# Last graphs of a graph network: biases carried as a matrix row, first product by groups ahead of the last gates, another order of the final operations

## The reference, cut to what matters

```python
A = (adj != 0)
h = x
for l in range(5):                      # block one: message passing and a GRU
    m = h @ weight[l]
    agg = einsum('bij,bid->bjd', A, m)
    h = gru_cell(agg, h, w_ih, w_hh, b_ih, b_hh)   # h' = (1-z)*n + z*h
x = layernorm(x + h * mask)

fused = 0                               # block two: only nodes 0..24 of a graph
for g, idx in enumerate(GROUPS):        # five groups of node numbers below 25
    adj_g = adj[:, idx][:, :, idx]      # normalised by degrees in graph_conv
    h1  = relu(norm_adj @ (x[:, idx] @ W1[g]) + b1[g])
    out = relu(norm_adj @ (h1 @ W2[g]) + b2[g])
    fused[:, idx] += softmax(fusion_w)[g] * out
out = layernorm(x + fused)
```

## Time and profile before

| quantity | value |
|---|---|
| median of 3 runs | 494.8 us (494.42 to 495.2) |
| the profiled execution's own time | 494.57 us |
| its span, first to last instruction | 492.8 us |
| mean granted PE clock | 0.997 |
| PE busy | 482.4 us (98%) |
| DVE, ACT, POOL busy | 352.5, 303.3, 334.8 us |

### The profile page before, as it was taken

The page is one execution under the profiler, slowest core; times in us unless marked ns, Lnnn a source line. Parts: engine busy times, 40 slices in busy tenths (PEclk is TensorE's granted clock), DMA queues, the critical chain, the costliest instruction groups (busy, mean ns, idle before and its releaser), DMA issues.

```text
span 492.8 us, 7184 instructions
## 1 busy us (share of the span) xinstructions
PE 482.4 (98%) x2305; PEld 230.2 (47%) x2305; DVE 352.5 (72%) x663; ACT 303.3 (62%) x536; POOL 334.8 (68%) x378
## 2 busy tenths in 40 slices
PE   7999999999999999999999999999999999999995
PEld 5344444444444444444444444444444444564564
DVE  3777867696866687778687768868668675445796
ACT  4556655655655566777667776576755767645555
POOL 3654774748775598997689658659996766234466
PEclk9999999999999999999999999999999999999998
DMA  8878252665535447264955486223443233322313
GB/s 269 257 172 159 45 150 55 175 160 129 119 68 156 108 95 185 51 140 105 184 112 154 113 196 179 66 51 82 97 100 75 48 65 67 65 38 44 80 45 86
DMA packets 133732, 55.97 MB, mean 114 GB/s; under 512 B 97257, under 2 KB 125374, under 8 KB 133694
## 3 DMA queue, kind: packets, MB, share of 16 engines
q1 hardware_dynamic: 108316, 32.39, 32.3%
q10 hardware_dynamic: 25378, 23.12, 15.3%
HBM read 27.70 MB, written 4.19 MB: 65 GB/s over the span
## 4 chain that ended last, share of the span: by engine, by line
PE 82%; POOL 6%; DMA 4%; DVE 3%; issue 2%; ACT 2%; SPq 0%; POOLq 0%; DVEq 0%; ACTq 0%
PE pA L779 24%; PE pR L784 6%; PE pR L786 6%; PE pR L785 6%; PE pZ L786 6%; PE pZ L785 6%; PE pZ L784 6%; PE pIN L784 3%; PE pHN L784 3%; PE pIN L786 3%; PE pHN L785 3%; PE pIN L785 3%; PE pHN L786 3%; POOL ZH L515 2%; DMA HT<-NAT 1%
## 5 line engine op out<-in xcount | busy, mean ns | idle before, releaser
L526 POOL TENSOR_TENSOR HT<-H,HT 128x512 f16<-128x512 f32 x76 | 91.8, 1208 | 91.4 <-ACT HT L1149 91.4
L779 PE MATMUL pA<-A,NAT 128*128 128x512 fp8e4 x640 | 151.0, 379 | 0.0
L515 POOL TENSOR_TENSOR ZH<-Z,H 128x512 f32<-128x512 f32 (+1 forms) x80 | 102.6, 1282 | 28.7 <-ACT Z L1164 27.4
L1389 DVE SCALAR_TENSOR_TENSOR T<-pHN,BHN,R 128x512 f32<-128x512 f32 (+1 forms) x80 | 59.9, 748 | 78.5 <-ACT R L1156 78.1
L1169 ACT ACTIVATE pIN<-T,COLS 128x512 f32<-128x512 f32 (+1 forms) x80 | 55.3, 691 | 71.7 <-DVE T L1393 71.6
L779 PEld LDWEIGHTS pA<-A,NAT 128*128 128x128 f16 x640 | 62.3, 98 | 75.3 <-issue 1.5
L1149 ACT ACTIVATE HT<-H 128x512 f16<-128x512 f32 x76 | 47.8, 629 | 64.6 <-DVE H L1403 64.4
L1399 DVE SCALAR_TENSOR_TENSOR pIN<-Z,pIN 128x512 f32<-128x512 f32 (+1 forms) x80 | 55.1, 688 | 24.5 <-ACT pIN L1169 24.3
L1156 ACT ACTIVATE R<-pR,BRZ 128x512 f32<-128x512 f32 (+1 forms) x80 | 54.3, 679 | 22.4 <-PE pR L786 21.5
L1403 DVE TENSOR_TENSOR H<-ZH,pIN 128x512 f32<-128x512 f32 (+1 forms) x80 | 54.8, 685 | 10.0 <-POOL ZH L515 7.6
L1383 DVE TENSOR_TENSOR AG<-pA,AG 128x512 f16<-128x512 f32 x80 | 54.7, 684 | 8.1 <-ACT AG L1145 8.1
(11 more groups left out here) (288 smaller groups left out, 813.9 us busy)
## 6 DMA issues: line engine op xcount, KB each, us to landing
AS<-in_adj_dram ACTq DMA_DIRECT2D x13, 1024.0 KB, 5.9
XR<-in_x_dram ACTq DMA_DIRECT2D x16, 256.0 KB, 2.9
XS<-in_x_dram ACTq DMA_DIRECT2D x13, 256.0 KB, 3.6
out_dram<-Y SPq DMA_DIRECT2D x16, 192.0 KB, 2.3
AS<-in_adj_dram SPq DMA_DIRECT2D x2, 1024.0 KB, 8.8
AS<-in_adj_dram SPq DMA_DIRECT2D x4, 256.0 KB, 5.5
NAT<-HT SPq DMA_TRANSPOSE x64, 3.1
XS<-in_x_dram SPq DMA_DIRECT2D x3, 256.0 KB, 7.8
```

What stands on the lines that cost most here:

```text
L515: g_.tensor_tensor(ZH[:, cs], Z[:, cs], H[:, b, cs], ALU.mult).then_inc(zh_p, 1)
L526: g_.tensor_tensor(HT[:, b, 1, :], H[:, b, :], HT[:, b, 0, :], ALU.subtract).then_inc(h_lo, 1)
L779: last = mm(pA2[:, k % 2, :], NAT[:, k % 2, h, i, :], A8[:, b, i, :], start=(h == 0 and i == 0), stop=(h == 1 and i == NI - 1))
L1389: v.scalar_tensor_tensor(out=T[:, cs], in0=pHN[:, cs], scalar=BHN[:, 0:1], in1=R[:, cs], op0=ALU.add, op1=ALU.mult).then_inc(t_v, 1)
```

## The change

- **Biases.** `B2S` and `biases` go. The unused partition rows 96 to 127 of `S2` get the biases of `W2`'s layer in step 13; row 121 (`LAST_BIAS_ROW`) alone is kept, scaled with the fusion weight. `read_s` writes rows 0 to 120 only. A new matrix `BDT` is the adjacency plus, in row 121, the group's membership; it is made on DVE in step 40 by five operations. `conv_d` uses it.
- **Second stage by groups.** `conv_b(0)` does groups 0 to 2 for both hidden halves (6 matmuls for 5) and stands in PE's step 79 right behind the pHN product, ahead of the state's pR and pZ products. `conv_b(1)` does groups 3 and 4 (4 for 5). ACT's `read_b(0)` moves ahead of the reset gate of step 79.
- **Order of the end.** On PE, back(14) stands behind all the gates of step 79, and back(15) behind the whole first `conv_s`. On ACT, two blocks of graph 12 are normalised between the update gate and the tanh of step 79; graph 13's two between the two `read_s`. On DVE, scales(12) goes to step 79 and scales(13) ahead of new_state(79); scales(14) ahead of variances(15); `stats_z` behind scales(15) and normalise(15). `variances` has one operation less (L1471) and the POOL roots 4 elements for 5. On POOL, graph 13's blocks 0 and 1 are normalised instead of 2 and 3. The first store of graph 15 no longer waits for ACT.

```diff
@@ SP, store_y
-                sp.wait_ge(f_on, b + 1)
...
-                sp.dma_start(out[b, S:P, :], Y[S:P, b % 4, 0, :]).then_inc(st_y[b % 4], 16)
+                if b == B - 1:
+
+                    sp.dma_start(out[b, S:P, :], Y[S:P, b % 4, 0, :]).then_inc(st_y[b % 4], 16)
+                sp.wait_ge(f_on, b + 1)
+                if b < B - 1:
+                    sp.dma_start(out[b, S:P, :], Y[S:P, b % 4, 0, :]).then_inc(st_y[b % 4], 16)
@@ POOL
-                g_.tensor_tensor(RS[:, w, :], VE[:, w, :], NHALF[:, 0:NI + 1], ALU.pow).then_inc(f_rs, 1)
+                g_.tensor_tensor(RS[:, w, 0:NI], VE[:, w, 0:NI], NHALF[:, 0:NI], ALU.pow).then_inc(f_rs, 1)
...
             residual(B - 2)
+            pool.wait_ge(f_nb, E0 + 2)
             normalise(E0, range(2))
             inverse_root(B - 2)
-            normalise(E0 + 1, range(2, NI))
+            normalise(E0 + 1, range(2))
             inverse_root(B - 1)
@@ PE, gates_of_state
                 split_product(pHN[:, cs], WH[:, 0, 2, :], WH[:, 1, 2, :], ht[0], ht[1], True, True)
+                if k == K - 1:
+
+                    conv_b(0, LAST_BANKS[1])
                 if k > 0:
                     pe.wait_ge(sig_r, k)
                 split_product(pR[:, cs], WH[:, 0, 0, :], WH[:, 1, 0, :], ht[0], ht[1], True, False)
@@ PE
+            def conv_b(part, bank):
+                groups = LAST_PARTS[part]
+                n = COL[groups.stop] - COL[groups.start]
+                if part == 0:
+                    pe.wait_ge(c_ea, 1)
+                for g in range(groups.start, groups.stop):
+                    for h in range(NH):
+                        at = h * n + COL[g] - COL[groups.start]
+                        last = mm(bank[:, at:at + COL[g + 1] - COL[g]], W1S[:, g, h * P:(h + 1) * P],
+                                  YT[:, COL[g]:COL[g + 1]], start=True, stop=True)
                 last.then_inc(c_mm, 1)
@@ PE, the end
+            back(B - 2)
             conv_b(1, LAST_BANKS[2])
-            pe.wait_ge(sig_r, K)
-            biases(LAST_PARTS[0], LAST_BANKS[5][:, 0:3 * D])
-            pe.wait_ge(sig_z, K)
-            biases(LAST_PARTS[1], LAST_BANKS[6][:, 0:2 * D])
             pe.wait_ge(f_ym, B - 1)
             mm(FUT, IDF[:, :], X1[:, TAIL, :], start=True, stop=False)
+            pe.wait_ge(c_ea, 2)
+            conv_s(range(0, 3), LAST_BANKS[3])
+            back(B - 1)
             pe.wait_ge(c_ea, 3)
-            conv_s(range(0, 3), LAST_BANKS[3], lambda: back(B - 1))
             conv_s(range(3, G), LAST_BANKS[4])
+            pe.wait_ge(b2_v, 2)
+            pe.wait_ge(sig_r, K)
             pe.wait_ge(c_ea, 4)
-            conv_d(TAIL, range(0, 3), LAST_BANKS[5], True)
+            conv_d(range(0, 3), LAST_BANKS[5])
@@ ACT, step 79 and the end
                     read_a(TAIL, LAST_BANKS[0])
+                    read_b(0, LAST_BANKS[1])
                 reset_gate(k)
                 update_gate(k)
...
-                    read_b(TAIL, 0, LAST_BANKS[1])
+                    normalise(E0, range(2, NI))
                 new_gate(k)
...
+            act.wait_ge(b2_v, 1)
+            read_s(0)
+            normalise(E0 + 1, range(2, NI))
+            read_s(1)
+            read_d(0)
+            read_d(1)
             normalise(B - 2, range(2))
             normalise(B - 1, range(2, NI))
@@ DVE
+            def last_matrices():
+                dve.wait_ge(bd_p, BD_STEPS - 1)
+                for g in range(G):
+                    last = v.scalar_tensor_tensor(out=BDT[:, g, :, :], in0=CM[:, g:g + 1, :].to_broadcast([P, Q, S]),
+                                                  scalar=IDF[:, LAST_BIAS_ROW:LAST_BIAS_ROW + 1],
+                                                  in1=BD[:, g, TAIL, :, :], op0=ALU.mult, op1=ALU.add)
+                last.then_inc(b2_v, 1)
...
                 if k == EARLY + 1:
                     stats(E0 + 1)
+                    scales(E0)
...
             masked(B - 2)
+            scales(E0 + 1)
             new_state(K - 1)
-            scales(B - 4)
-            scales(B - 3)
             stats(B - 2)
             masked_residual(B - 1)
-            stats(B - 1)
+            dve.wait_ge(f_mv, B - 1)
+            stats_of_rows(B - 1)
             scales(B - 2)
+            variances(B - 1)
             normalise(B - 2, range(2, NI))
-            stats_z()
             scales(B - 1)
             normalise(B - 1, range(2))
+            stats_z()
             normalise_z()
```

More of the change, by code:

```diff
@@ L107 @@
 assert BIAS_ROW < S
+LAST_BIAS_ROW = P - S + BIAS_ROW
 assert ROWS_OF == [S] + [S // 2] * (G - 1)
@@ L195, in graph_net_kernel @@
         W2S = sb("W2S", [P, G, NH, D], F32)
-        B2S = sb("B2S", [P, G, D], F32)
+        BDT = sb("BDT", [P, G, Q, S], F32)
         YT = sb("YT", [P, COL[G]], F32)
@@ L346, in graph_net_kernel @@
         f_rs = sem("f_rs")
+        z_p = sem("z_p")
         f_nb = sem("f_nb")
@@ L740, in _ @@
             residual(B - 2)
+            pool.wait_ge(f_nb, E0 + 2)
             normalise(E0, range(2))
             inverse_root(B - 2)
-            normalise(E0 + 1, range(2, NI))
+            normalise(E0 + 1, range(2))
             inverse_root(B - 1)
-            inverse_root_z()
+            pool.wait_ge(z_v, 3)
+            g_.tensor_tensor(RS[:, 4 + TAIL, 0:1], VE[:, 4 + TAIL, 0:1], NHALF[:, 0:1], ALU.pow).then_inc(z_p, 1)
         @block.tensor
@@ L786, in split_product, with gates_of_state @@
                 return mm(bank, w_lo, v_hi, start=False, stop=stop)
-            def gates_of_state(k, between=lambda: None):
+            def gates_of_state(k):
                 b = GRAPH[k]
@@ L802, in gates_of_state @@
                 split_product(pR[:, cs], WH[:, 0, 0, :], WH[:, 1, 0, :], ht[0], ht[1], True, False)
-                between()
                 if k > 0:
@@ L823, in first_gates_of_state, with gates_of_messages @@
                 split_product(pZ[:, :], WH[:, 0, 1, :], WH[:, 1, 1, :], hi, lo, True, False)
-            def gates_of_messages(k, between=lambda: None):
+            def gates_of_messages(k):
                 l, cs = LAYER[k], COLS_OF[k]
@@ L895, in conv_a, with conv_s @@
                    BD[:, 1:G, c, :, 0:S // 2], start=True, stop=True).then_inc(c_mm, 1)
[L897 to L900, removed]
+            def conv_b(part, bank):
[8 more added lines that the diff above has]
+                                  YT[:, COL[g]:COL[g + 1]], start=True, stop=True)
                 last.then_inc(c_mm, 1)
-            def conv_s(groups, bank, behind_first=lambda: None):
+            def conv_s(groups, bank):
                 for j, g in enumerate(groups):
@@ L907, in conv_s, with conv_d @@
                                   start=(h == 0), stop=(h == NH - 1))
-                    if j == 0:
-                        behind_first()
                 last.then_inc(c_mm, 1)
-            def conv_d(c, groups, bank, biased=False):
+            def conv_d(groups, bank):
                 for j, g in enumerate(groups):
-                    last = mm(bank[:, j * P:(j + 1) * P], BD[:, g, c, :, :].rearrange("p q n -> p (q n)"), S2[:, g, :],
-                              start=not biased, stop=not biased or j == len(groups) - 1)
+                    last = mm(bank[:, j * P:(j + 1) * P], BDT[:, g, :, :].rearrange("p q n -> p (q n)"), S2[:, g, :],
+                              start=True, stop=True)
                 last.then_inc(c_mm, 1)
@@ L922, in conv_sum @@
                     last.then_inc(c_mm, 1)
-            def biases(groups, bank):
-                pe.wait_ge(b2_v, 1)
-                mm(bank, IDF[:, :], B2S[:, groups, :].rearrange("p g e -> p (g e)"), start=True, stop=False)
             wide = [t[:, 0:TAIL * P].rearrange("p (c x) -> p c x", c=TAIL) for t in (pC, pF)]
@@ L1052, in _ @@
                     back(E0 + 1)
[L1053 to L1058, removed]
+                gates_of_messages(k)
                 if k <= 2:
                     aggregate(k + 1)
+            back(B - 2)
             conv_b(1, LAST_BANKS[2])
-            pe.wait_ge(sig_r, K)
-            biases(LAST_PARTS[0], LAST_BANKS[5][:, 0:3 * D])
-            pe.wait_ge(sig_z, K)
-            biases(LAST_PARTS[1], LAST_BANKS[6][:, 0:2 * D])
             pe.wait_ge(f_ym, B - 1)
             mm(FUT, IDF[:, :], X1[:, TAIL, :], start=True, stop=False)
+            pe.wait_ge(c_ea, 2)
+            conv_s(range(0, 3), LAST_BANKS[3])
+            back(B - 1)
             pe.wait_ge(c_ea, 3)
-            conv_s(range(0, 3), LAST_BANKS[3], lambda: back(B - 1))
             conv_s(range(3, G), LAST_BANKS[4])
+            pe.wait_ge(b2_v, 2)
+            pe.wait_ge(sig_r, K)
             pe.wait_ge(c_ea, 4)
-            conv_d(TAIL, range(0, 3), LAST_BANKS[5], True)
+            conv_d(range(0, 3), LAST_BANKS[5])
+            pe.wait_ge(sig_z, K)
             pe.wait_ge(c_ea, 5)
-            conv_d(TAIL, range(3, G), LAST_BANKS[6], True)
+            conv_d(range(3, G), LAST_BANKS[6])
```

(36 more changed lines are left out.)

9 lines of the change are left out of this document (2 added, 7 removed).

## The result

The changed kernel takes 498.4 us (median of 5 runs, 498.1 to 499.74), the kernel before, beside it, 494.9 us. The ratio is 1.0073, with a 95% interval of 1.0055 to 1.009: it is slower by 0.7%, 3.5 us. 495.8 had been forecast, within 494.6 to 496.8. The profiled execution took 498.1.

The account below looks back on a forecast made before the run. PE was taken to bound up to step 79, then a POOL chain to graph 15's store. ZO's issue at 490.7 plus 3.1 gave 493.8 against 492.8, +1.0 us (0.7 stall, 0.3 order): median 495.8, range 494.6 to 496.8.

Parts of the forecast that it names:

- Part 1: PE in step 79: conv_b(0) ahead of the gates waits 1.0 us for YT; R +1.21 us, L1393 +0.96.
- Part 2, biases: Removed bias matmuls, 1.1 us of PE, lie in its wait for ACT's relu and are worth nothing on the path.
- Part 2, step 40: Five added DVE operations in step 40 take 1.4 us, 2.8 as upper end; hidden, so 0 on the path.
- the cover: Slack in step 40 between H(40) being ready, some 250.7, and PE wanting it at 250.82: 0.1 us.
- step 40 isn't covered: Rival: H(40) late by up to 1.4 us stalls PE or delays step 79's tanh, +0.5 to +1.4; chance 0.15.
- The rule that the prediction quoted for VE(14): DVE and GpSimd share an exclusively locked port pair; the loser waits a whole instruction, making VE(14) 0.1 us later.
- Part 3: POOL's roots near the end: of the 1.0 us delay only 0.35 is left when root(15) ends, at 488.16.
- Part 4: End of kernel: stats_z behind normalise(15) makes ZO's store issue 1.7 us later, at 490.7, and last, taking 3.1 us.
- the stall: PE's wait for YT in step 79 as a share of the forecast sum: 0.7 us.
- the order: Placing stats_z behind scales(15) and normalise(15), as a share of the forecast sum: 0.3 us.

Follow-up runs that it names:

- e8: The kernel before with only the bias row (matrices in step 72, no bias matmuls) and the 4-element POOL roots: 494.85 us against 494.99.
- e1: The changed kernel with the five matrix operations in step 72 instead of step 40: 496.0 us against 494.83 for the kernel before.
- e10: The changed kernel with the five matrix operations in step 48 instead of step 40: 495.66 us against 494.65 for the kernel before.
- e7: The changed kernel with two of the five matrix operations in step 40 and three in step 72: 497.19 us against 494.99 for the kernel before.
- e9: The changed kernel with the matrices in step 72 and five one-input bn_stats on the same data in step 40: 496.19 us against 494.65 for the kernel before.
- e5: e1 with ACT's read_a ahead of the tanh of step 78 instead of behind it: 494.94 us against 494.99 for the kernel before.
- e4: The changed kernel with stats_z ahead of scales(15) and normalise(15): 498.77 us against 494.83 for the kernel before.
- e6: e5 with stats_z ahead of scales(15) and normalise(15): 494.26 us against 494.99 for the kernel before.
- e11: The kernel of e6 run once more for a narrower interval: 494.38 us against 494.65 for the kernel before.

## Why the prediction was wrong, point by point

- **Part 1** held. PE's wait for YT was forecast at 1.0 us, its rows give 0.83 to 1.3. R was to start 1.21 us later: from pHN of step 79 it is 481.18 - 476.17 = 5.01 us, before 477.39 - 473.69 = 3.70, so +1.31. L1407 came 1.03 later on the same scale, +0.96 was said, and directly behind L1403, not behind pIN.
- **Part 2, biases**: held (e8). **Part 2, step 40, is the step that failed:** "five operations of 128x128. The nearest rows are L1497, 1.12 for four, so 1.4 us, and the doubled case 2.8 as the upper end." And: "I take 0; the cover is 0.1 us, and the ends are 0 and 1.4 us." The 0 was 2.64 us, and both halves of the step were wrong. The price came from an operation with one input in PSUM, which POOL didn't hold, although it ran beside it from 483.84 on. For operations that POOL leaves alone it was right: in e1 and e10 the five took 1.76 us with one of them held for 0.37. In step 40 they took 3.37, above even the doubled case. The rows to take were the earlier trace rows and the first of the earlier trace rows: the masking in that very step takes 1.18 us beside POOL with both inputs in SBUF, where 0.68 is usual with one in PSUM. With these rows, two blocked operations of 1.3 and three of 0.34 make 3.6 us; 3.37 was measured, since the records overlap. The second half, the cover, was counted for PE alone, where it held (1.5 us). A delay of H(40) also goes through ACT to POOL, whose queue is full up to ZH(44), and is charged in step 45: 1.3 us of PE's wait in e7 (1.0 of it by POOL's delay), 0.5 in e9, both with no wait in step 41. The rival "step 40 isn't covered", at +0.5 to +1.4 and a chance of 0.15, named the place and had less than the size.
- The rule that the prediction quoted for VE(14) was the one that decided this term, and it was not applied there. The Trainium skill, SBUF - State Buffer, section "SBUF: two separate sides", names among what GpSimd blocks also DVE operations "with two SBUF inputs". The runs agree: 1.35 against 0.34 us in the changed kernel, 0.27 for the one-input bn_stats in e9.
- **Part 3** came out 0.2 us short. root(15) ended at 490.88, 14.71 from pHN; before 14.12; +0.59, where +0.35 was said. The 4-element root takes 1.01 to 1.10 (1.04 said). VE(15) waited for normalise(13) a second time (0.31 us instead of 0.17), as part 3 describes for VE(14), and normalise(13) took 1.59 (1.5 said).
- **Part 4** held: ZO's store was issued 1.79 us later on that scale (+1.7 said), ended 2.99 us after (3.1 said), and was last. That the last stretch came out at +1.02 with +1.0 said is in part luck: root(15) was 0.24 later than said, while the way from it to ZO's issue and the store itself were 0.1 shorter each.
- **How the sum splits**: 0.7 for the stall and 0.3 for the order had been said. Taking away the stall gave 1.1 (e5), putting stats_z back 0.3 to 0.6 (e4, e6, e11). Together they are more than the +1.0 us: with both out (e6, e11) the end is 0.3 to 0.4 shorter than before. Which of the other moves gives that was not measured one by one.

## What to carry to other kernels

Price an operation by its kind, by where its inputs lie, and by what runs on GpSimd beside it, not by its size alone; a small operation beside a busy GpSimd took four times its own time here (1.35 us for 0.34). When work is put into a steady pipeline, the reserve of the bottleneck engine is one of several: follow the delay to every engine that the late result feeds, and ask when that engine next has idle time. Cut traces at instructions that both kernels have before comparing; whole times hid 0.6 us here behind a start that varied by over 1 us.

## What the runs showed of the hardware that was not expected

- One POOL operation held up a DVE operation with two SBUF inputs, and the next POOL operation held up the next DVE one: in step 40, 1.35 and 1.30 us in a row, the fourth and fifth at 0.34 again. Between the two POOL operations DVE got one operation through. With one input in PSUM, DVE ran at its usual 0.68 us beside the same POOL operation.
- The stretch from the start to step 7, with the initial loads, took 55.3 to 57.7 us in thirteen profiled executions of kernels that hardly differ there; step 7 to step 79 repeated within 0.12 us in the seven in which PE had no new wait in it (417.88 to 418.00).
